# A two-layer state-space image network on one core: another order of work in the tails after the scan

## What is computed

```
# layer 0
y = y * jax.nn.silu(z)
out = jnp.einsum('bhwe,de->bhwd', y, out_proj_w)
t = jax.nn.relu(bn(jnp.einsum('bhwc,oc->bhwo', y, e1_w) + e1_b, ...))
t = jax.nn.relu(bn(depthwise_conv(t, e2_w, e2_b, 1), ...))
t = jnp.einsum('bhwc,oc->bhwo', t, e3_w) + e3_b
s = jax.nn.sigmoid(jax.nn.relu(jnp.mean(t, axis=(1, 2)) @ se1_w.T + se1_b) @ se2_w.T + se2_b)
return out + t * s[:, None, None, :]
# layer 1
mu = y.mean(-1, keepdims=True); var = y.var(-1, keepdims=True)
y = (y - mu) * lax.rsqrt(var + 1e-05) * out_norm_g + out_norm_b
return (y * jax.nn.silu(z)) @ out_proj_w.T
```

## Time and profile before

| | us |
|---|---|
| median of 3 runs (lowest, highest) | 27117.58 (27114.8, 27121.14) |
| the profiled execution | 27120.91 |
| its span, first to last instruction | 27119.1 |
| busy: PE, DVE, ACT, POOL | 24625.3 (91%), 24462.1 (90%), 22561.4 (83%), 20690.0 (76%) |
| mean granted clock of TensorE | 0.967 of full speed |

### The profile page before, as it was taken

One profiled execution on the slowest core, in us unless ns is written; L12 is line 12 of the kernel. 1 busy time (PEld: TensorE's weight loads), 2 busy tenths in 40 slices (PEclk: granted clock), 3 DMA queues, 4 the chain that ended last, 5 costly groups with the idle time before them and its releaser, 6 DMA issues.

```text
span 27119.1 us, 389769 instructions
## 1 busy us (share of the span) xinstructions
PE 24625.3 (91%) x96900; PEld 13618.6 (50%) x96900; DVE 24462.1 (90%) x17385; ACT 22561.4 (83%) x52277; POOL 20690.0 (76%) x12084
## 2 busy tenths in 40 slices
PE   8999998999999999999989999999999899999999
PEld 4455554555445554555445554445554445544455
DVE  8888988899888998889888999888998988998989
ACT  8777987788777887789778898888988888988888
POOL 8677976778677876778667887777887777977778
PEclk9999999999999999999999999999999999999999
DMA  4443543444443444345434454444544444544444
GB/s 153 124 128 127 166 126 126 128 139 155 124 127 128 158 135 126 127 134 160 126 122 139 147 160 136 136 136 138 160 147 136 137 138 138 169 136 136 137 139 147
DMA packets 1414979, 3764.21 MB, mean 139 GB/s; under 512 B 205408, under 2 KB 205536, under 8 KB 1412064
## 3 DMA queue, kind: packets, MB, share of 16 engines
q1 hardware_dynamic: 1412448, 3736.17, 43.5%
HBM read 3659.85 MB, written 47.19 MB: 137 GB/s over the span
## 4 chain that ended last, share of the span: by engine, by line
PE 33%; issue 23%; DVE 22%; ACT 18%; POOL 3%; DVEq 0%; ACTq 0%; DMA 0%; POOLq 0%; SPq 0%
PE ps L800 13%; DVE ps L1419 8%; DVE arena L1424 8%; ACT arena L1201 8%; ACT arena L1135 4%; PE ps L768 4%; DVE arena L564 3%; PE ps L620 2%; POOL arena L1547 2%; PE ps L788 2%; PE ps L679 1%; PE ps L805 1%; PE ps L806 1%; PE ps L644 1%; PE ps L657 1%
## 5 line engine op out<-in xcount | busy, mean ns | idle before, releaser
L1547 POOL TENSOR_TENSOR arena<-arena 128x768 f32<-128x768 f32 x9216 | 16561.6, 1822 | 1540.1 <-DVE arena L1424 1326.7
L800 PE MATMUL ps<-arena,consts 128*128 128x384 f32 x36864 | 13657.3, 494 | 332.2 <-ACT arena L1235 160.2
L1424 DVE TENSOR_TENSOR_SCAN arena<-arena,carry,ps 128x768 f32<-128x768 f32 x6144 | 10910.4, 1805 | 417.7 <-PE ps L768 262.1
L1135 ACT ACTIVATE arena<-arena,An 128x768 f32<-128x768 f32 x9216 | 8446.3, 930 | 525.8 <-POOL arena L1547 516.7
L800 PEld LDWEIGHTS ps<-arena,consts 128*128 128x128 f32 x36864 | 6329.3, 191 | 4047.0 <-issue 430.9
L1424 DVE TENSOR_TENSOR_SCAN arena<-arena,ps 128x768 f32<-128x768 f32 x3072 | 5286.9, 1746 | 395.2 <-PE ps L768 296.2
L1419 DVE TENSOR_TENSOR ps<-ps,arena 128x768 f32<-128x768 f32 x5216 | 4921.1, 943 | 386.0 <-PE ps L788 381.3
L1201 ACT ACTIVATE arena<-arena 128x64 f32<-128x64 f32 (+1 forms) x14976 | 4266.7, 367 | 583.4 <-PE ps L768 557.0
L768 PE MATMUL ps<-consts,arena 128*128 128x128 f32 x24000 | 3388.7, 278 | 976.5 <-DVE arena L1424 743.8
L1201 ACT ACTIVATE arena<-arena,bT 128x64 f32<-128x64 f32 (+1 forms) x14592 | 4169.6, 368 | 95.9 <-PE ps L768 74.2
L768 PEld LDWEIGHTS ps<-consts,arena 128*128 128x128 f32 x24000 | 2753.5, 142 | 2809.6 <-issue 1678.7
(11 more groups left out here) (184 smaller groups left out, 19541.2 us busy)
## 6 DMA issues: line engine op xcount, KB each, us to landing
arena<-c_rows SPq DMA_DIRECT2D x6144, 384.0 KB, 3.8
arena<-c_rows SPq DMA_DIRECT2D x6144, 192.0 KB, 3.5
arena<-arena SPq DMA_DIRECT2D x384, 72.0 KB, 2.6
c_rows<-arena SPq DMA_DIRECT2D x96, 192.0 KB, 3.1
arena<-x SPq DMA_DIRECT2D x17, 864.0 KB, 4.5
...
```

Source lines behind the costliest of these rows:

```text
L800: mm = pe.matmul(y_part[:, h, :], ident, hC[it % NH][:, h * SEG:(h + 1) * SEG], start=(n == 0), stop=(n == NS - 1))
L1135: act.activation(state_at[it % NW], delta[g % 2], ACT.Exp, scale=An[:, slot(s) * NS + n:slot(s) * NS + n + 1]).then_inc(sem["da_ready"], 1)
L1424: dve.tensor_tensor_scan(a[:, ::back], a[:, ::back], slots[it % 2][:, ::back], 0.0 if k == 0 else carry[:, n:n + 1], ALU.mult, ALU.add).th ...
L1547: pool.tensor_tensor(hC[it % NH], state_at[it % NW], Csb[b], ALU.mult).then_inc(sem["hc_ready"], 1)
```

## The change

It has four parts. (1) In layer 0 the sums of groups 15 and 16 (counted from 0) go through ACT's copy like all others; at the start of the tail DVE gates their two thirds of the image with one SBUF instruction of 128 x 1536, and then the last group's sums out of PSUM. (2) In every projection and mean with two weight tiles PE takes three segments with the first tile and then three with the second. (3) In `norm` PE's second shift unit moves behind the variances, and DVE's order is: variance of x, gate, both reciprocals, then product and shift of both halves, then `ln_apply`; ACT's square of x moves between the squares of y, its table load behind them, and `ln_root` to the end. (4) In `branch` the whole of `norm_x(1)` moves ahead of the depthwise convolution on DVE, and ACT's parts of it (with one more table load) to the start.

```
@@ -600,7 +600,8 @@
     for first, end, name, n in [
-            (U_MU, U_SHIFT, "mu_taken", 2), (U_SHIFT, U_VAR, "shift_kept", 1), (U_VAR, U_OUT, "ysd_kept", 1),
+            (U_MU, U_SHIFT, "mu_taken", 2), (U_SHIFT, U_VAR, "shift_kept", 1), (U_VAR, U_SHIFT_1, "ysd_kept", 1),
+            (U_SHIFT_1, U_OUT, "shift_kept", 2),
             (U_OUT, U_OUT_T, "o_scaled", 1), (U_OUT_T, q, "x1_ready", 1)]:
@@ -912,6 +913,7 @@
             pe.matmul(segs(k, (0, DM))[:, g, :], w_out[:, 0, :], in_order(yg[0], h, g), start=True, stop=False)
+        for g in range(3):
             mm = pe.matmul(segs(k, (0, DM))[:, g, :], w_out[0:DB, 1, :], in_order(yg[1], h, g), start=False, stop=True)
@@ -957,24 +959,13 @@
     for h in range(2):
-        k = U_MU + h
-        claim(k)
-        for g in range(3):
-            cols = slice(h * HALF + g * SEG, h * HALF + (g + 1) * SEG)
-            pe.matmul(segs(k)[:, g, :], mean_w, yg[0][:, cols], start=True, stop=False)
-            mm = pe.matmul(segs(k)[:, g, :], mean_w[0:DB, :], yg[1][:, cols], start=False, stop=True)
-        mm.then_inc(sem["unit_full"], 1)
+        means(U_MU + h, mean_w, yg, P, h)
     pe.wait_ge(sem["sz_ready"], v("sz_ready", 2))
-    for h in range(2):
-        out_proj(U_SHIFT + h, sz, 1, h)
-    for h in range(2):
-        k = U_VAR + h
-        claim(k)
+    out_proj(U_SHIFT, sz, 1, 0)
+    for h in range(2):
         pe.wait_ge(sem["y_squared"], v("y_squared", 2 * h + 2))
-        for g in range(3):
-            pe.matmul(segs(k, (0, DM))[:, g, :], mean_w[:, 0:DM], in_order(ysq[0], h, g), start=True, stop=False)
-            mm = pe.matmul(segs(k, (0, DM))[:, g, :], mean_w[0:DB, 0:DM], in_order(ysq[1], h, g), start=False, stop=True)
-        mm.then_inc(sem["unit_full"], 1)
+        means(U_VAR + h, mean_w[:, 0:DM], ysq, DM, h)
+    out_proj(U_SHIFT_1, sz, 1, 1)
     pe.wait_ge(sem["gated"], v("gated", 4))
@@ -982,12 +973,22 @@
     transpose_x(1)
+
+def means(k, w, src, m, h):
+
+    claim(k)
+    for g in range(3):
+        pe.matmul(segs(k, (0, m))[:, g, :], w, in_order(src[0], h, g), start=True, stop=False)
+    for g in range(3):
+        mm = pe.matmul(segs(k, (0, m))[:, g, :], w[0:DB, :], in_order(src[1][0:DB, :], h, g), start=False, stop=True)
+    mm.then_inc(sem["unit_full"], 1)

...
         pe.matmul(segs(k, (0, DM))[:, g, :], wgb[:, q, 0, :], in_order(src[0], h, g), start=True, stop=False)
+    for g in range(3):
         mm = pe.matmul(segs(k, (0, DM))[:, g, :], wgb[0:DB, q, 1, :], in_order(src[1][0:DB, :], h, g), start=False, stop=True)
@@ -1229,7 +1230,7 @@
     s, p, j, k, c = group(g)
-    if At.layer == 0 and g >= NG - NC:
+    if At.layer == 0 and g == NG - 1:
         return
@@ -1263,20 +1264,21 @@
     gates()
-    nc.scalar.preload_act_table_set("sqrt_and_others")
-    ln_square(act, "in", ALL, at=1)
     for h in range(2):
...
             act.activation(ysq[t][:, cols], yg[t][:, cols], ACT.Square).then_inc(sem["y_squared"], 1)
-    for h in range(2):
-        keep_unit(U_SHIFT, shift_T, "shift_kept", h)
-    ln_root(act, "in", ALL, at=1)
+        if h == 0:
+            ln_square(act, "in", ALL, at=1)
+    nc.scalar.preload_act_table_set("sqrt_and_others")
+    keep_unit(U_SHIFT, shift_T, "shift_kept", 0)
     for h in range(2):
...
                        ACT.Sqrt, bias=se[0:DM, 15:16]).then_inc(sem["ysd_kept"], 1)
+    keep_unit(U_SHIFT_1 - 1, shift_T, "shift_kept", 1)
+    ln_root(act, "in", ALL, at=1)
     keep_xT(1, range(5))
@@ -1297,6 +1301,8 @@
             i.then_inc(sem["t1_ready"], 1)
+            if t == 0 and h == 0:
+                ln_root(act, "in", ALL, at=1)
     nc.scalar.preload_act_table_set("sigmoid_and_others")
@@ -1423,17 +1427,16 @@
                                0.0 if k == 0 else carry[:, n:n + 1], ALU.mult, ALU.add).then_inc(sem["scanned"], 1)
-        if At.layer == 0 and n == 4 and g > NG - NC:
-            gate_sums(g - 1)
         if At.layer == 0 and n == STEP_AT["gate"] and 0 <= g - FIRST_MERGE < NC:
...

-def gate_sums(g):
-
-    c = group(g)[4]
+def gate_sums():
+
     dve.wait_ge(sem["sz_ready"], v("sz_ready", 2))
-    dve.wait_ge(sem["y_summed"], v("y_summed", NS * (g + 1)))
-    dve.tensor_tensor(halves(chunk(yg[0], c)), y_part, halves(chunk(sz[0], c)), ALU.mult).then_inc(sem["y_gated"], 1)
+    dve.wait_ge(sem["y_moved"], v("y_moved", NG - 1))
+    dve.tensor_tensor(yg[0][:, CH:], yg[0][:, CH:], sz[0][:, CH:], ALU.mult).then_inc(sem["y_gated"], 1)
+    dve.wait_ge(sem["y_summed"], v("y_summed", NIT))
+    dve.tensor_tensor(halves(chunk(yg[0], 0)), y_part, halves(chunk(sz[0], 0)), ALU.mult).then_inc(sem["y_gated"], 1)
@@ -1444,7 +1447,7 @@
     if layer == 0:
-        gate_sums(NG - 1)
+        gate_sums()
     else:
@@ -1470,12 +1473,11 @@
 def branch():
+    norm_x(1)
     for n, t in enumerate(E2_ORDER):
...
         depthwise(dve, t1[t], wcol("e2")[:, 9 * t:9 * t + 9], t2[t][:, start * W:], "e2_tap", 9 * n, start, H, start)
-    ln_center(dve, "in", xin, ALL, lambda c: dve.wait_ge(sem["x_loaded"], v("x_loaded", 32)), at=1)
-    ln_spread(dve, "in", EPS_IN, 0, ALL[0], at=1)
     dve.wait_ge(sem["se_ready"], v("se_ready", 1))
@@ -1483,7 +1485,6 @@
             .then_inc(sem["br_scaled"], 1)
-    ln_apply(dve, "in", xc, 0, ALL[0], at=1)
     for h in range(2):
@@ -1498,22 +1499,25 @@
             dve.tensor_tensor(o, o, segs(k, (0, m)), ALU.subtract).then_inc(sem["mu_taken"], 1)
+    ln_spread(dve, "in", EPS_IN, 0, ALL[0], at=1)
     dve.wait_ge(sem["sz_ready"], v("sz_ready", 2))
...
         dve.tensor_tensor(yg[t], yg[t], sz[t][0:(P, DB)[t], :], ALU.mult).then_inc(sem["gated"], 2)
-    ln_scale(dve, "in", EPS_IN, xc, ALL, at=1)
+    for h in range(2):
+        cols = slice(h * HALF, (h + 1) * HALF)
+        dve.wait_ge(sem["ysd_kept"], v("ysd_kept", h + 1))
+        dve.reciprocal(yrstd_T[:, cols], yrstd_T[:, cols]).then_inc(sem["yrstd_ready"], 1)
     for h in range(2):
...
         by_seg = [a[:, cols].rearrange("p (g x) -> p g x", g=3) for a in (out_T, yrstd_T)]
-        dve.wait_ge(sem["ysd_kept"], v("ysd_kept", h + 1))
-        dve.reciprocal(yrstd_T[:, cols], yrstd_T[:, cols]).then_inc(sem["yrstd_ready"], 1)
         dve.wait_ge(sem["yrstd_ready"], v("yrstd_ready", h + 1))
...
         dve.tensor_tensor(out_T[:, cols], out_T[:, cols], shift_T[:, cols], ALU.add).then_inc(sem["o_shifted"], 1)
+    ln_apply(dve, "in", xc, 0, ALL[0], at=1)
     for h in range(2):
```

More of the change, by code:

```diff
@@ L158 @@
     "duT_full": NG, "duT_ready": NG, "bT_full": PAIRS + 1, "bT_ready": PAIRS + 1, "scanned": NIT, "hc_ready": NIT, "y_summed": NIT,
[L159 removed]
+    "y_moved": (NG - 1, NG), "y_gated": (2, 0),
     "z_ready": len(Z_UNITS), "z_copied": len(Z_UNITS), "sz_ready": 2, "merge_ready": NC, "merge_taken": NC, "gated": (0, 4),
@@ L572, in metaformer @@
         U_E1, U_CV, U_YG, U_BR, U_BR_T = 7, 13, 15, 17, 19
-        U_MU, U_SHIFT, U_VAR, U_OUT, U_OUT_T = 7, 9, 11, 13, 15
+        U_MU, U_SHIFT, U_VAR, U_SHIFT_1, U_OUT, U_OUT_T = 7, 9, 10, 12, 13, 15
         U_Q = (21, 17)
@@ L812, in emptied @@
             def emptied(g):
-                if At.layer == 0 and g >= NG - NC:
-                    pe.wait_ge(sem["y_gated"], v("y_gated", g + 1 - (NG - NC)))
+                if At.layer == 0 and g == NG - 1:
+                    pe.wait_ge(sem["y_gated"], v("y_gated", 2))
                 else:
@@ L1599, in body @@
                 if layer == 0:
-                    pool.wait_ge(sem["y_gated"], v("y_gated", NC))
+                    pool.wait_ge(sem["y_gated"], v("y_gated", 2))
                     hold(pool)
```

1 line of the change is left out of this document (removed).

## The result

| | before | after |
|---|---|---|
| median (runs) | 27119.2 us (4) | 26841.3 us (4) |
| lowest to highest | 27114.8 to 27121.1 | 26834.0 to 26853.7 |
| profiled execution, its span | 27120.9, 27119.1 | 26838.6, 26836.8 |

The ratio is 0.9898, with a 95% interval of 0.9881 to 0.9915: 278 us less, where 292 were forecast. The time lies in the range, and in the likeliest case's own range too.

What follows compares the result with a forecast made beforehand. No engine alone was taken to bound the kernel, but the waits between engines. Parts of 120 + 146 + 26 = 292 us off 27117.6 gave 26826 us, 1.08% less; range 26785 to 26885.

Steps and rivals of the forecast that it cites:

- the likeliest case's own range: Whole kernel: the forecast of 26826 us, chance 79%, with its own range of 26798 to 26865 us.
- Part 1, 120 us: Layer 0's groups 16 and 17: PE's wait behind DVE's gate becomes layer 1's, 7.5 us for each of 16 images.
- So it costs nothing: Start of layer 0's tail: the new wide gate, some 1.7 us, stands where DVE waits for PE's last sums.
- Parts 2 and 3, 146 us: Layer 1's tail: grouped weight tiles and the new order start PE's transposes 9.1 us earlier in each of 16 images.
- The walk through the three engines: Layer 1's tail: the new order followed on PE, DVE and ACT from 14691.76; DVE's last instruction ends at 730.1, before 739.2.
- The share without the grouping: Layer 1's tail: the new order with units still 5.04 and 4.88 us gains 5.3 us instead of 9.1.
- Part 4, 26 us: Layer 0's tail: normalising the next x before the convolution brings the merge earlier, 1.6 us for each of 16 images.
- the lower bound: Layer 0's tail: part 4 gains 0 if PE's clock falls at the last e3 unit, for which the merge waits.
- the convolution starts 0 to 0.3 us later: Layer 0's tail: normalising x, about 10.7 us, goes into DVE's gap of 10.52 us before the depthwise convolution.
- Slower by the clock in layer 1's row of eight units: Rival, layer 1's tail: at PE's lower clock units take 8.4 us, the last shift ends 22.6 later; 27334 us, chance 3%.
- The sums' stall: Rival, layer 0: ACT's copy comes late or the wait moves, so part 1 brings nothing; 26946 us, chance 4%.
- The clock taking part of the rest: Rival, layer 0's e1 units and small chain: PE's clock shifts up to 30 us either way; 8% for leaving the range.

## Why the prediction was right, and where not

- **Part 1, 120 us.** Groups 16 and 17 fell by 7.58 us on the mean of 15 images (forecast 7.5) and the whole of the scans by 7.39, so 118 us; alone the part brought 112. "So it costs nothing", of the wide gate, was wrong by a little: DVE's time was covered, as said, but the gate ran beside POOL's last product, which took 3.24 us instead of 1.81, and the last gate came 0.26 us later, 4 us in all. The Trainium skill, page "GPSIMD Engine Reference", section "1. Specifications", says that GpSimd's SBUF interfaces are shared with VectorE and contended by DVE instructions with two SBUF inputs; by that rule the trace agrees: the gate has two, and the product that took 3.24 us beside it took 1.81 when the gate waited. DVE paid nothing for it (1.73 beside the product, 1.76 alone).
- **Parts 2 and 3, 146 us.** The transposes came 9.08 us earlier (forecast 9.1), 145 us, and the next image 9.27, 148. The walk through the three engines held at each step within 0.4 us: from the first mean the gate began after 13.7 us (forecast 13.3), the reciprocals after 18.6 (18.3) and the last shift ended after 38.4 (38.3). The share without the grouping held too (84 us, forecast 85). The grouping on the old order brought 4.6 us at the transposes and not the rest, 3.8, so in layer 1 the two parts overlap. That the height costs and not the tile was shown by the means at one height.
- **Part 4, 26 us.** Here the size was off: 1.37 us at the transposes (forecast 1.6), 0.87 at the next image's first scan, so 14 us. Counted from the convolution the merge came 1.78 us earlier (forecast 1.75), so the small chain was costed rightly, and the error lies before and behind it. The prediction named one cause as the lower bound, a fall of PE's clock, but looked for it at the last e3 unit; it fell behind the following wait for the merge, and filling that wait gave layer 0 1.73 us an image back. The other loss is at the front: "the convolution starts 0 to 0.3 us later" came to 0.51. Of it 0.26 is the late gate; the rest is e1's slow start in 15 of 16 images instead of 12. With both mended the convolution starts at 18.16, 0.16 behind the 18.0 of an image of before with a fast e1, so DVE's own chain was costed rightly. POOL's work on the diagonals did not delay it, though nine of them took 6.72 us and not 5.4 (0.766 us each against 0.605).
- **The rivals.** Slower by the clock in layer 1's row of eight units: no, 1.00 up to the last unit, as in the last of its windows, at the end of this section. The sums' stall: no. The clock taking part of the rest: yes, with the sign against the change. Part 4 came out 12 us short; 4 of them are the gate beside POOL's product, which no rival had, so some 8 are left for the clock. All of it is inside the forecast's own range. That the total came within 14 us is in part luck: 11 of layer 1's 15 stretches gained 10.35 us on the mean, 1.25 above the 9.1 forecast, and the four slow ones took that back.

```profile
14584.00:14591.00 7.00, 7.00 (x21) 2.86 (x20) 7.00 (x2) 1.23 (x2) 0.00 (x0) 1.00 0.00 0
```
